# Combining of groups nine units apart instead of eleven, deeper rings for stored rows and weights, first units between the last products

## The chip, the cores and the metric

One Trainium2 chip, of which the kernel uses one core. The metric is the device time of one execution in microseconds (us), from the runtime's own count; a profiled execution also has a span, from its first to its last instruction. The engines of the core are named as the profile names them: PE (TensorE), DVE (VectorE), ACT (ScalarE), POOL (GpSimd) and SP (SyncE, which here only issues transfers).

## The reference

Inputs are x (8192 x 128) and adj (8192 x 8192), all float32. A layer norm of x goes through a graph layer whose weights are a function of adj, and the result through a mixture of 16 experts of which each row takes two.

```python
def _L0_gnn_ref(z, dist_matrix, W, B):
    msg = z @ W + B
    sens = sensitivity(dist_matrix, MU, SIGMA)      # exp(-(1/r - 1/mu)**2 / (2 sigma**2))
    weights = jnp.where(dist_matrix < CUTOFF, sens, 0.0)
    return weights @ msg

def _L0_ffn_ref(x, gate_w, gate_b, w1, b1, w2, b2, gamma, beta):   # E=16, K=2, H=128, F=256
    gate_logits = x @ gate_w + gate_b
    topk_vals, topk_idx = jax.lax.top_k(gate_logits, K)
    topk_w = jax.nn.softmax(topk_vals, axis=-1)
    h = jax.nn.relu(jnp.einsum('bsh,ehf->bsef', x, w1) + b1)
    expert_out = jnp.einsum('bsef,efh->bseh', h, w2) + b2
    sel = jnp.take_along_axis(expert_out, topk_idx[:, :, :, None], axis=2)
    y = x + jnp.sum(topk_w[..., None] * sel, axis=2)
    return layernorm(y) * gamma + beta

x = x + _L0_gnn_ref(_layernorm(x), adj, L0_gnn_W, L0_gnn_B)
x = x + _L0_ffn_ref(_layernorm(x)[None], ...)[0]
```

## The kernel before

The 8192 rows are 16 groups of 512. **The graph stage** takes group after group: 16 chunks of adj (512 rows x 512 columns, 1 MB) go through a ring of 8 buffers; DVE masks and squares (L614, L620), ACT takes a logarithm and an exponential (L488, L493), PE turns the chunk (L1078), ACT writes the weights (L499), and `products` on PE (L1059) adds weights times messages into one PSUM bank, two steps (`BEHIND`) after the turn. Two steps make a chunk, 32 a group. While a group runs, the gate of the group before is computed in slots between the steps (`gate_slot`): a second layer norm, the gate's logits, the two best experts, the row that each pair (row, expert) gets in a table sorted by expert, and eight indirect DMAs on POOL (L454) that scatter the normalised rows to `rows_in`.

**The expert stage** follows for all groups. The sorted rows are cut into 188 units of 128 rows, each of one expert, in four batches (63, 55, 39 and 31 units, of 6, 5, 3 and 2 groups). Unit `u` goes through these steps, each an in-order queue of its engine:

- SP `load_rows` (L352) reads its 64 KB from `rows_in`, 14 units ahead (`RIN`).
- DVE `fetch` (L923) copies the expert's first weights out of the resident table into one of `SLOTS` buffers, `AHEAD` units ahead; every 16 units it first reads the experts' numbers into registers (a TENSOR_LOAD, L917).
- PE `turn_tile` (L1097), four units ahead; ACT `copy_rows` (L552); PE `hidden` (L1108), two ahead; ACT `relu_hidden` (L561); PE `output` (L1136); DVE `add_bias` (L932), which writes the result into one of `RO` buffers, each for a pair of units; SP `store_rows` (L365) stores a pair (128 KB) to `rows_out`. `add_bias` of a pair waits until the store that last used its buffer has landed.

**Combining** brings the results back, a group at a time. POOL gathers the group's rows with eight indirect DMAs (L472) into one of 4 buffers; it begins a batch's first group when all stores of that batch have landed. SP reads the kept rows of the group (L376). `combine_slot(g, m)` then does ten steps m = 0 to 9 on DVE and ACT, one per unit, behind the unit's own instructions in the same queues: two weighted additions on DVE (L947, four instructions each), statistics (L626, L633), a reciprocal root (ACT L505, L507, and DVE L641 to L645), a shift (L961), the scaling on ACT (L573, four instructions), gamma (L966) and the last addition (L971). SP stores the group (L380).

**What sets the order.** Every engine runs one loop over `i`; unit `i`'s instructions come first and then those of `combine_slot(g, i - starts[g])`. `starts` is a list computed once: a group starts no earlier than `COMBINE_WAIT` = 14 units after its batch, and no earlier than `COMBINE_PACE` units after the group before. With 11 that gives 77, 88, 99, 110, 121, 132, 143, 154, 165, 176, 187, 198, 209, 220, 231, 242. Iterations from 188 on have no units in them, only combining.

```python
starts.append(max(at, starts[-1] + COMBINE_PACE) if starts else at)   # at = UNIT0[b + 1] + COMBINE_WAIT
```

The last products of the graph stage (steps 30 and 31 of group 15) stand on PE ahead of the first turns and hidden layers of the units. DVE's first fetches stand ahead of `gate_sum` (L706), which copies the last sum out of PSUM.

## Time and profile before

| | us |
|---|---|
| median of three runs | 1753.15 (1749.15 to 1754.33) |
| the profiled execution, its own time | 1751.72 |
| its span | 1750.0 |
| last turn of the graph stage on PE begins | 1466.33 |
| first unit's output on PE begins | 1475.57 |
| first combining begins | 1559.71 |
| last unit's bias begins | 1697.90 |
| last combining begins | 1738.76 |

Busy shares over the whole span are PE 92%, DVE 87%, ACT 91% and POOL 29%; they are averages over a graph stage of some 1470 us, which the change leaves alone up to its last two steps, and an expert stage of some 280 us. Times in the trace count from the span's start. A row of the timeline has its start, its length, the engine, the line, the operation with what it writes and reads, the number of merged instructions, and in brackets how long its engine was idle before it and what ended that. Names such as `chunk` and `msg` stand for the memory in which the expert stage's buffers are carved (`ro`, `slots`, `rin`, `back`, `zs`, `fin` in chunk; `rT`, `hT` in msg).

### The profile page before, as it was taken

How to read it: one execution, taken by the hardware profiler on the slowest of the kernel's cores; microseconds unless marked ns; L12 is line 12 of the kernel's file. 1: busy time of each engine (PE TensorE's matmuls, PEld its weight loads, DVE VectorE, ACT ScalarE, POOL GpSimd, SP SyncE). 2: the span in 40 equal slices, each digit the busy share in tenths (PEclk: the TensorE clock that was granted, in tenths of full speed). 3: DMA queues.
4: the chain of work that ended last, by engine and by line, in shares of the span. 5: the costliest groups of instructions: out<-in, count | busy, mean ns of one | idle time of the engine just before them, and what ended most of it. 6: DMA issues, size and time to landing. Idle time of an engine off the chain costs nothing.

```text
span 1750.0 us, 25339 instructions
## 1 busy us (share of the span) xinstructions
PE 1615.9 (92%) x8350; PEld 1074.9 (61%) x8350; DVE 1524.9 (87%) x2435; ACT 1598.6 (91%) x1749; POOL 514.8 (29%) x344
## 2 busy tenths in 40 slices
PE   4889999999999998999999999999999989998970
PEld 3556666666656565666665656556666656997860
DVE  7999989899999999989899999998989894576876
ACT  5889999999999999899999999989999986786862
POOL 1001040404041415050505050505050512156773
PEclk9999999999999999999999999999999999999995
DMA  9447876766666667576666676756676742466762
GB/s 320 146 139 251 247 212 197 218 197 209 200 203 200 203 201 217 172 216 198 205 198 211 196 214 192 225 171 209 198 216 197 225 118 61 134 171 192 203 169 83
DMA packets 228927, 338.30 MB, mean 193 GB/s; under 512 B 19200, under 2 KB 86272, under 8 KB 228672
## 3 DMA queue, kind: packets, MB, share of 16 engines
q1 hardware_dynamic: 220480, 319.63, 61.8%
q0 software_dynamic: 8320, 17.06, 3.3%
q8 instruction: 70, 1.15, 0.3%
q14 instruction: 57, 0.47, 0.1%
HBM read 303.07 MB, written 33.55 MB: 192 GB/s over the span
## 4 chain that ended last, share of the span: by engine, by line
PE 50%; ACT 21%; DVE 18%; issue 7%; POOL 2%; DMA 1%; DVEq 0%; SPq 0%; ACTq 0%; POOLq 0%
PE acc L1059 26%; PE tp L1078 13%; ACT chunk L488 8%; ACT chunk L493 6%; DVE chunk L614 6%; DVE chunk L620 5%; ACT wT L499 5%; PE tp L1108 4%; PE tp L1136 2%; PE acc L1136 2%; POOL spread L442 2%; DVE stats L626 2%; PE tp L1097 1%; DVE chunk L947 1%; PE misc L1011 1%
## 5 line engine op out<-in xcount | busy, mean ns | idle before, releaser
L1059 PE MATMUL acc<-wT,msg 128*128 128x512 f32 x2048 | 972.2, 597 | 0.0
L499 ACT ACTIVATE wT<-tp 128x1024 f32<-128x1024 f32 x512 | 751.8, 1468 | 30.3 <-PE tp L1078 30.2
L620 DVE SCALAR_TENSOR_TENSOR chunk<-chunk 128x2048 f32<-128x2048 f32 x256 | 584.8, 2284 | 65.6 <-ACT chunk L493 65.2
L1078 PEld LDWEIGHTS tp<-ident,chunk 128*128 128x128 f32 x4096 | 481.4, 142 | 224.7 <-issue 214.2
L488 ACT ACTIVATE chunk<-chunk 128x2048 f32<-128x2048 f32 x256 | 604.1, 2360 | 11.9 <-DVE chunk L614 11.9
L493 ACT ACTIVATE chunk<-chunk 128x2048 f32<-128x2048 f32 x256 | 605.8, 2367 | 0.0
L614 DVE SCALAR_TENSOR_TENSOR chunk<-chunk 128x2048 f32<-128x2048 f32 x256 | 583.8, 2281 | 2.3 <-DMA chunk<-in_adj_dram 2.3
L1078 PE MATMUL tp<-ident,chunk 128*128 128x128 f32 x4096 | 535.7, 274 | 0.0
L1059 PEld LDWEIGHTS acc<-wT,msg 128*128 128x128 f32 x2048 | 351.1, 191 | 252.8 <-issue 249.7
L454 POOL DMA_INDIRECT rows_in<-y,row_now x128 | 281.8, 2202 | 44.6 <-issue 44.6
L435 POOL TENSOR_TENSOR pool_carrier<-pool_carrier 1x1 f32<-1x1 f32 x32 | 10.3, 323 | 730.1 <-DVE row_now L791 707.8
L442 POOL TENSOR_SCALAR spread<-mv_now 128x4 f32<-128x4 f32 x16 | 53.4, 3339 | 394.8 <-DVE mv_now L633 394.8
L561 ACT ACTIVATE msg<-tp,chunk 128x128 f32<-128x128 f32 x376 | 117.8, 367 | 26.5 <-PE tp L1108 25.6
L472 POOL DMA_INDIRECT chunk<-rows_out,row_back x128 | 125.2, 978 | 39.1 <-issue 36.6
L1108 PE MATMUL tp<-msg,chunk 128*128 128x128 f32 x752 | 115.9, 277 | 0.0
L1108 PEld LDWEIGHTS tp<-msg,chunk 128*128 128x128 f32 x752 | 99.8, 193 | 0.0
L552 ACT ACTIVATE msg<-tp 128x128 f32<-128x128 f32 x188 | 51.9, 277 | 25.7 <-PE tp L1097 25.1
L923 DVE COPY chunk<-blobs 128x258 f32 x188 | 56.7, 304 | 17.7 <-ACT msg L561 14.8
L1136 PE MATMUL acc<-blobs,msg 128*128 x376 | 60.3, 283 | 9.6 <-DVE chunk L932 7.0
L1136 PE MATMUL tp<-blobs,msg 128*128 x376 | 60.6, 284 | 8.8 <-ACT msg L561 4.6
L1136 PEld LDWEIGHTS acc<-blobs,msg 128*128 128x128 f32 x376 | 49.8, 193 | 13.4 <-issue 12.6
L1136 PEld LDWEIGHTS tp<-blobs,msg 128*128 128x128 f32 x376 | 50.2, 194 | 12.6 <-issue 12.1
(112 smaller groups left out, 740.5 us busy)
## 6 DMA issues: line engine op xcount, KB each, us to landing
chunk<-in_adj_dram SPq DMA_DIRECT2D x256, 1024.0 KB, 5.4
chunk<-rows_in SPq DMA_DIRECT2D x188, 64.0 KB
rows_out<-chunk SPq DMA_DIRECT2D x92, 128.0 KB
y_kept<-y SPq DMA_DIRECT2D x16, 256.0 KB, 6.1
rows_in<-zeros SPq DMA_DIRECT2D x64, 64.0 KB
chunk<-y_kept SPq DMA_DIRECT2D x16, 256.0 KB
out_dram<-chunk SPq DMA_DIRECT2D x16, 256.0 KB, 2.7
blobs<-in_L_ffn_w_dram SPq DMA_DIRECT2D x1, 2048.0 KB, 11.7
```

The lines of the kernel that those rows point to most:

```text
L454: pool.indirect_dma_start(rows_in, bass.IndirectOffsetOnAxis(row_now[:, k, b:b + 1].bitcast(U32), 0), y[:, b, :], None).then_inc(scattered ...
L472: pool.indirect_dma_start(back[g % BACK][:, kb, :], None, rows_out[b], bass.IndirectOffsetOnAxis(row_back[:, g, kb:kb + 1].bitcast(U32), 0 ...
L488: act.activation(slot(c), slot(c), ACT.Ln, bias=TINY).then_inc(logged, 1)
L493: act.activation(slot(c), slot(c), ACT.Exp, scale=-1.0).then_inc(inverted, 1)
L499: act.activation(wT[:, (g * PPG + m) % WSLOTS, :], tp[(g * PPG + m) % TSLOTS][:, :], ACT.Exp, scale=-2.0).then_inc(weighted, 1)
L561: ins = act.activation(hT[u % HT][:, t * n:(t + 1) * n], h_bank[u % H_BANKS][:, t * n:(t + 1) * n], ACT.Relu, bias=slots[u % SLOTS][:, B1 ...
L614: dve.scalar_tensor_tensor(out=slot(c), in0=slot(c), scalar=1.0, in1=slot(c), op0=ALU.is_lt, op1=ALU.mult).then_inc(masked, 1)
L620: dve.scalar_tensor_tensor(out=slot(c), in0=slot(c), scalar=2.0, in1=slot(c), op0=ALU.subtract, op1=ALU.mult).then_inc(squared, 1)
L1059: ins = pe.matmul(acc[:, :], msg[:, n, :], wT[:, (g * PPG + m) % WSLOTS, k * ROWS:(k + 1) * ROWS], start=(n == 0), stop=(n == 2 * PPG - 1))
L1078: ins = pe.transpose(tp[s % TSLOTS][:, t * ROWS + b * P:t * ROWS + (b + 1) * P], chunk[:, c % RING, b, j:j + P], ident[:, :])
L1108: ins = pe.matmul(h_bank[u % H_BANKS][:, t * n:(t + 1) * n], slots[u % SLOTS][:, W1 + t * P:W1 + (t + 1) * P], rT[u % RT][:, 0:n], start=T ...
L1136: ins = pe.matmul(o_bank[u % O_BANKS][:, r:r + D], hT[u % HT][:, t * n + r:t * n + r + P], blobs[:, bass.ds(second_layers[u], 1), W2 + t * ...
```

## The change

Four constants and the place of two pieces of work:

- `COMBINE_PACE` goes from 11 to 9. `starts` becomes 77, 86, 95, 104, 113, 122, 132, 141, 150, 159, 168, 177, 186, 195, 204, 213. SP's loads of the kept rows (at `starts[g] - COMBINE_PACE`) come nine units ahead instead of eleven.
- `RO` goes from 4 to 8 pairs of stored rows, `SLOTS` from 9 to 12 and `AHEAD` from 7 to 8.
- On PE, the products of the last two steps stand between the turns of units 0 to 3 and the hidden layers of units 0 and 1.

```diff
-        SLOTS, RIN, RT, HT, RO, BACK, ZS, FIN = 9, 14, 4, 4, 4, 4, 3, 2
+        SLOTS, RIN, RT, HT, RO, BACK, ZS, FIN = 12, 14, 4, 4, 8, 4, 3, 2
...
-        AT_ONCE, AHEAD = 16, 7
+        AT_ONCE, AHEAD = 16, 8
...
-        COMBINE_WAIT, COMBINE_PACE, COMBINE_LONG = 14, 11, 10
+        COMBINE_WAIT, COMBINE_PACE, COMBINE_LONG = 14, 9, 10
...
-            for m in range(PPG - BEHIND, PPG):
-                products(GROUPS - 1, m)
-
...
-            for u in range(TURN_LEAD):
-                turn_tile(u)
-            for u in range(HIDDEN_LEAD):
-                hidden(u)
+            turn_tile(0)
+            turn_tile(1)
+            products(GROUPS - 1, PPG - 2)
+            turn_tile(2)
+            turn_tile(3)
+            hidden(0)
+            products(GROUPS - 1, PPG - 1)
+            hidden(1)
```

PE at the seam of the two stages, before: after the last turn (L1078) all six remaining products (L1059), then four turns of units (L1097), the hidden layers of two (L1108, two instructions each), unit 4's turn and unit 2's hidden layer.

```order
1129 L1078 MATMUL tp<-ident,chunk 128x128 x8
1130 L1059 MATMUL acc<-wT,msg 128x512 x6
1131 L1097 MATMUL tp<-ident,chunk 128x128 x4
1132 L1108 MATMUL tp<-msg,chunk 128x128 x4
1133 L1097 MATMUL tp<-ident,chunk 128x128
1134 L1108 MATMUL tp<-msg,chunk 128x128 x2
```

PE at the same place in the changed kernel, where L1097 has become L1094 and L1108 L1105:

```order
1129 L1078 MATMUL tp<-ident,chunk 128x128 x8
1130 L1059 MATMUL acc<-wT,msg 128x512 x2
1131 L1094 MATMUL tp<-ident,chunk 128x128 x2
1132 L1059 MATMUL acc<-wT,msg 128x512 x2
1133 L1094 MATMUL tp<-ident,chunk 128x128 x2
1134 L1105 MATMUL tp<-msg,chunk 128x128 x2
1135 L1059 MATMUL acc<-wT,msg 128x512 x2
1136 L1105 MATMUL tp<-msg,chunk 128x128 x2
```

The four turns and the first hidden layer moved ahead of the last products; the second hidden layer stands behind them as before.

DVE between two groups' combining late in the stage (groups 8 and 9), before: the last step of one group (L971), two more units' bias (L932) and fetch (L923), then the first step of the next group (L947).

```order
2020 L971 TENSOR_TENSOR chunk<-chunk,xs 128x512
2021 L932 ISA
2022 L932 TENSOR_TENSOR chunk<-tp,blobs 128x128
2023 L923 ISA
2024 L923 COPY chunk<-blobs 128x258
2025 L932 ISA
2026 L932 TENSOR_TENSOR chunk<-acc,blobs 128x128
2027 L923 ISA
2028 L923 COPY chunk<-blobs 128x258
2029 L947 SCALAR_TENSOR_TENSOR chunk<-chunk,share 128x128 x4
```

DVE in the changed kernel, between groups 9 and 10:

```order
2003 L966 TENSOR_TENSOR chunk<-chunk,gamma_bc 128x512
2004 L932 ISA
2005 L932 TENSOR_TENSOR chunk<-acc,blobs 128x128
2006 L917 TENSOR_LOAD e_tab
2007 L923 ISA
2008 L923 COPY chunk<-blobs 128x258
2009 L971 TENSOR_TENSOR chunk<-chunk,xs 128x512
2010 L947 SCALAR_TENSOR_TENSOR chunk<-chunk,share 128x128 x4
```

The last step of a group and the first of the next now stand in the same unit's place, with no unit between them that carries no combining. At the end of the loop, three whole groups (13, 14 and 15) stand behind the last unit instead of five.

## Rows read from the trace of the kernel before

**Rows 1.** Busy time by stage: start:end, us, then each engine's busy us
```profile
1475.50:1560.00 84.50, 82.55 (x723) 81.21 (x724) 50.75 (x227) 65.85 (x235) 19.01 (x23) 1.00 0.48 136
1560.00:1697.00 137.00, 120.85 (x974) 114.06 (x973) 100.89 (x444) 105.71 (x381) 99.63 (x112) 0.98 0.71 193
```
**Rows 2.** Timeline of DVE: the first step of groups 0 to 4, 10 and 15
```profile
1559.71 1.14 DVE L947 SCALAR_TENSOR_TENSOR chunk<-chunk,share 128x128 f32<-128x128 f32 x4 [0.50 <-DMA chunk<-rows_out,row_back]
...
1572.44 1.12 DVE L947 SCALAR_TENSOR_TENSOR chunk<-chunk,share 128x128 f32<-128x128 f32 x4
...
1590.99 1.13 DVE L947 SCALAR_TENSOR_TENSOR chunk<-chunk,share 128x128 f32<-128x128 f32 x4
...
1603.19 1.13 DVE L947 SCALAR_TENSOR_TENSOR chunk<-chunk,share 128x128 f32<-128x128 f32 x4
...
1621.38 1.12 DVE L947 SCALAR_TENSOR_TENSOR chunk<-chunk,share 128x128 f32<-128x128 f32 x4
...
1696.86 1.13 DVE L947 SCALAR_TENSOR_TENSOR chunk<-chunk,share 128x128 f32<-128x128 f32 x4
...
1738.76 2.31 DVE L947 SCALAR_TENSOR_TENSOR chunk<-chunk,share 128x128 f32<-128x128 f32 x8
```
**Rows 3.** Timeline at the end: last unit's bias and store, last step of group 15
```profile
1697.90 0.28 DVE L932 TENSOR_TENSOR chunk<-acc,blobs 128x128 f32<-128x128 f32 x1
...
1698.49 0.47 SPq L365 DMA_DIRECT2D rows_out<-chunk  x1
...
1746.49 0.69 DVE L971 TENSOR_TENSOR chunk<-chunk,xs 128x512 f32<-128x512 f32 x1
```
**Rows 4.** Timeline of POOL: last gather of group 0, batches two and four
```profile
1556.94 0.94 POOL L472 DMA_INDIRECT chunk<-rows_out,row_back  x1 [0.30 <-issue]
...
1618.47 0.18 POOL L435 TENSOR_TENSOR pool_carrier<-pool_carrier 1x1 f32<-1x1 f32 x1 [8.54 <-DMA rows_out<-chunk]
...
1700.43 0.94 POOL L472 DMA_INDIRECT chunk<-rows_out,row_back  x1 [0.30 <-issue]
1702.78 0.18 POOL L435 TENSOR_TENSOR pool_carrier<-pool_carrier 1x1 f32<-1x1 f32 x1 [1.41 <-DMA rows_out<-chunk]
...
1724.51 0.94 POOL L472 DMA_INDIRECT chunk<-rows_out,row_back  x1 [0.30 <-issue]
```
**Rows 5.** Timeline of all engines at the seam, and two units behind it
```profile
1467.21 5.32 PE L1059 MATMUL acc<-wT,msg 128*128 128x512 f32 x12
...
1472.56 0.69 DVE L706 COPY yT<-acc 128x512 f32<-128x512 f32 x1 [10.90 <-PE acc L1059]
...
1475.57 0.71 PE L1136 MATMUL tp<-blobs,msg 128*128 x4 [0.50 <-ACT msg L561]
...
1483.12 0.61 PE L1136 MATMUL acc<-blobs,msg 128*128 x4
...
1484.12 0.61 PE L1136 MATMUL tp<-blobs,msg 128*128 x4
```
**Rows 6.** Who waited for whom, 1560 to 1697: us, times, longest
```profile
DVE chunk L966 <- ACT chunk L573: 8.4, 9, 1.3
DVE chunk L923 <- ACT msg L561: 8.2, 7, 3.1
DVE chunk L932 <- PE tp L1136: 6.9, 14, 1.3
...
DVE chunk L932 <- DMA rows_out<-chunk: 6.0, 2, 4.0
DVE chunk L932 <- PE acc L1136: 3.7, 9, 0.7
```
**Rows 7.** Timeline of DVE: a unit's bias that waited for a store
```profile
1586.74 0.29 DVE L932 TENSOR_TENSOR chunk<-acc,blobs 128x128 f32<-128x128 f32 x1 [4.01 <-DMA rows_out<-chunk]
...
1587.15 0.68 DVE L966 TENSOR_TENSOR chunk<-chunk,gamma_bc 128x512 f32<-128x512 f32 x1
```
**Rows 8.** DVE's register loads: duration in ns, minimum, median and longest
```profile
L917 DVEq TENSOR_LOAD <-e_tab x15: 310/1312/3654, 1458.3 to 1676.3; - x15
```

More of the change, by code:

```diff
@@ L1139, in output @@
                 ins.then_inc(o_full, 1)
-            for u in range(TURN_LEAD):
-                turn_tile(u)
-            for u in range(HIDDEN_LEAD):
-                hidden(u)
+            assert BEHIND == 2 and T_BANKS == 2 and TURN_LEAD == 4 and HIDDEN_LEAD == 2
+            turn_tile(0)
[6 more added lines that the diff above has]
+            hidden(1)
             for i in range(NU):
```

## The prediction, made before the changed kernel ran

> **What bounds the kernel now.** The change begins at the seam of the two stages, so I read the trace from there. First the busy time by stage [rows 1]. From the first unit to the first combining (77 units, 84.5 us) PE is busy 82.55 us: PE bounds, and an undisturbed unit takes 1.00 us, as two successive outputs show (1483.12, 1484.12) [rows 5]. From 1560 to 1697 the other 111 units share their queues with combining. There PE is busy 120.9 of 137 us, ACT 105.7, DVE 100.9 and POOL 99.6. No engine is full.
>
> Next the starts of groups [rows 2], which show the real pace. Eleven units take 12.73 us from group 0 to 1, 12.20 from 2 to 3, and on average (1696.86 - 1621.38) / 6 = 12.58 from 4 to 10: 12.58 / 11 = 1.144 us a unit. Two intervals stand out: 18.55 us from group 1 to 2 and 18.19 from 3 to 4. Then the table of waits for this stage [rows 6], which says what DVE, on which all combining hangs, waits for: ACT's scaling (8.4 us), something before a fetch (8.2), PE's outputs (6.9 + 3.7), and stores of rows (6.0 in two waits).
>
> Behind the last unit's bias (1697.90) come 52.1 us without PE [rows 3]. From group 10's start to group 15's are (1738.76 - 1696.86) / 5 = 8.38 us a group [rows 2]: one group's chain over DVE and ACT with nothing beside it. POOL finishes gathering group 15 at 1724.51 + 0.94 = 1725.45 [rows 4], but DVE takes it up at 1738.76. So the end is set by the chain of groups that are left over, not by gathers.
>
> **1. The seam.** Before, PE runs six product instructions in a row to 1467.21 + 5.32 = 1472.53, while ACT and DVE have nothing to do (DVE was idle for 10.90 us), and the first output starts at 1475.57 [rows 5], 3.04 us later. Now four turns and one hidden layer are inside the products. What PE must do behind the last product is hidden layer 1, turn 4, hidden layer 2. A unit is one turn and two pairs of matmuls in 1.00 us, so a turn is about 0.1 us and a pair about 0.45: 0.45 + 0.1 + 0.45 = 1.0 us. What moved ahead costs PE 4 x 0.1 + 0.45 = 0.85 us, by which the last product ends later. 3.04 - 0.85 - 1.0 = 1.2 us are saved at most, and nothing if a copy on ACT is late. The copies are 0.3 us pieces that have a product's 1.8 us to run in, so I take 1.1. The sum leaves PSUM 0.85 us later (L706), but the second output, which waits for it, comes after that anyway.
>
> **2. Deeper rings.** A bias waited 4.01 us for a store at 1586.74 [rows 7], and all such waits are 6.0 us [rows 6]. With four pairs a store has eight units to land; with eight it has sixteen. 6.0 us go. The check from elsewhere: the interval around them was 18.55 - 12.58 = 6.0 us too long. If the waits only move, it is 0. SLOTS and AHEAD I cost at nothing: the 8.2 us before fetches, for which the table names ACT, are the size of DVE's register loads, which last 1.31 us each and 3.65 at most [rows 8] and stay, in the same number. The eighth fetch (0.3 us) is covered by DVE's idle 10.90 us.
>
> **3. The pace inside the units.** 111 units held 10.1 groups at eleven apart and hold 12.3 at nine. What does a period of nine units cost? DVE: 100.9 / 10.1 = 10.0 us busy a period. Two units less take away 2 x 0.41 (1586.74 to 1587.15 is one bias and one fetch [rows 7]), which leaves 9.2. ACT's scaling keeps it waiting 8.4 / 10.1 = 0.8 us, register loads 8.2 / 10.1 x 9 / 11 = 0.7. Together 10.7 us. Its waits for PE (10.6 / 10.1 = 1.0 us) come on top or vanish, since DVE now runs with less slack. POOL: the eight groups 6 to 13 were gathered from 1618.47 to 1701.37, 10.36 us a group [rows 4], just under 10.7. PE needs 9.0, ACT less than DVE. So the bounds are 10.4 and 11.7, and I take 10.7 because DVE is nearest to full: 10.7 / 9 = 1.189 us a unit, 0.045 more than now, over 111 units **5.0 us lost** (2 to 17 between the bounds).
>
> The last bias starts at 1697.9 - 1.1 - 6.0 + 5.0 = 1695.8.
>
> **4. Behind the last unit.** Three whole groups are left, not five. DVE's chain alone would reach group 15 some 3 x 8.4 = 25 us after the last bias. But group 14 can't be gathered before the last stores land. POOL starts them at 1702.78, 4.9 us after the last bias, and is done at 1725.45, 22.7 us later [rows 4]. A gather lands some 1.8 us after its issue: group 0's last one ended its issue at 1557.88, and DVE, which waited for it, began at 1559.71 [rows 2, 4]. 4.9 + 22.7 + 1.8 = 29.4 us: what is late next is POOL, by 4 us over DVE's chain. From group 15's start to the end of the span are 1750.0 - 1738.76 = 11.2 us, as before. 29.4 + 11.2 = 40.6 instead of 52.1: **11.5 us saved**. Is POOL free by then? Group 13's gather ended 82.9 us after batch two's began; that beginning moves with the units to about 1612, so to 1695, before 1695.8 + 4.9.
>
> **The sum.** 1695.8 + 40.6 = 1736.4, that is 13.6 us less than 1750.0. Against the profiled execution's own time that is 1751.72 - 13.6 = 1738.1 us. Its time is 1.4 us below the median of the runs, so for the median 1739.5.
>
> **A rule of the Trainium skill that speaks against it.** The 128 gathers take POOL 0.94 us with 0.30 between them, the same beside units (1556.94) as in the tail, where no fetches run (1724.51) [rows 4]. The Trainium skill, "SBUF — State Buffer", section "SBUF: two separate sides", says of DMAs issued from GpSimd that a fp32 SBUF-to-SBUF copy on VectorE locks it out of the port they share, and puts such a DMA at about 3.1 us instead of 0.62. By it a denser DVE would stretch the gathers. The trace doesn't agree here, so the sum goes by the row.
>
> **The rivals.** *Combining doesn't overlap with units.* If DVE can do nothing useful in a group's chain, nine units cost 9 x 0.41 + 8.38 = 12.1 us, 1.341 a unit: 21.9 us lost in place of 5.0. The last bias comes at 1712.7, the span is 1753.3, and the median about 1756, slower than before. It decides from 11.8 us a period on, where the loss (18.6) eats all savings. Against it: by the same rule eleven units would cost 4.5 + 8.4 = 12.9, and three views of them gave 12.2 to 12.7. That is not far.
>
> *Gathers are held up by a busier DVE.* Let each wait for one DVE instruction of 0.28 us: 8 x 0.28 more is 12.6 us a group, and nine units can't go faster: 1.40 us a unit, 28 us lost instead of 5, and 2 x 2.2 more in the tail. The median would be about 1767. Against it stands the even 0.94.
>
> *The waits for stores stay.* Gathers, kept rows and results of a group are as many bytes in nine units as in eleven, so transfers are denser. If stores take that much longer, 6.0 us aren't saved: 1745.5.
>
> *The pace is nominal.* DVE keeps all its waits for PE, a period costs 11.1 to 11.7: 1744 to 1752.
>
> *More is gained.* The interval from group 3 to 4 was 5.6 us too long [rows 2], with the one register load of 3.65 us in it [rows 8]. If such a pause doesn't come again, or DVE and POOL run at 10.4 a period: 1731 to 1735.
>
> **How the numbers follow.** The forecast (1735 to 1744) gets 0.50, the nominal pace 0.17, the stores 0.10, more gained 0.15, no overlap 0.05, held-up gathers 0.03. The likeliest gives 1739.5. The range takes in the bounds of the pace, the stores and the gained pause: 1730 to 1749, which leaves out about 0.15. A measurement of this kernel can tell some 0.3% (5.3 us) from no change. Faster by more than that, below 1747.9: 0.91. Within it: 0.05. Slower: 0.04.
>
> **What would show it.** The first output starts 1.1 us earlier, with ACT's copies between products. No wait of a bias for a store is left. Groups start 10.4 to 11 us apart where they were 12.6. Behind the last bias DVE does two and a half groups and then waits some 4 us for the last gathers, which it never did; about 41 us lie between that bias and the end. I am wrong if periods are near 12, if the table of waits has DVE wait for gathers in the middle of batches, or if the clock that PE is granted falls in the unit stage for longer than before, which no term here has in it.

## The result, and the profile after

| | before | changed | ratio with its 95% interval |
|---|---|---|---|
| median of the runs, first comparison | 1751.68 us (6 runs) | 1745.18 us (6 runs) | 0.9961 [0.9947, 0.9974] |
| second comparison, another chip | 1750.90 us (11 runs) | 1745.43 us (6 runs) | 0.9966 [0.9954, 0.9978] |
| profiled execution: its own time | 1751.72 us | 1745.93 us | |
| its span | 1750.0 us | 1744.2 us | |

The changed kernel is faster by 6.5 us in the first comparison and by 5.5 us in the second: just more than the 0.3% that can be told from no change, and less than half of the 13.6 us that were forecast. The median lies inside the predicted range, 5.7 us above the forecast of 1739.5 and above the band of 1735 to 1744 that had most of the chance. The trace of the changed kernel tells which term took the rest, in the order of the prediction.

**The seam.** The timeline of all engines there (start, length, engine, line):

```profile
1465.05 1.04 PE L1078 MATMUL tp<-ident,chunk 128*128 128x128 f32 x8
...
1467.95 0.45 ACT L552 ACTIVATE msg<-tp 128x128 f32<-128x128 f32 x2 [0.81 <-PE tp L1094]
...
1470.24 1.88 PE L1059 MATMUL acc<-wT,msg 128*128 128x512 f32 x4
...
1472.96 0.61 PE L1133 MATMUL tp<-blobs,msg 128*128 x4
```

The second row is one of ACT's copies, now between products, the third is the last products, and the first output (fourth row) starts 7.91 us after the last turn of the stage before it; before it was 9.24 us. That is 1.3 us saved, where 1.1 was expected. The first bias comes 2.7 us earlier in all (1473.72 instead of 1476.42); the other 1.3 to 1.4 us were already there before the seam, in a part that the change doesn't touch, and are a difference between two executions.

**The unit stage.** The first steps of groups 0, 3, 4, 5, 6 and 12 on DVE, and the last bias:

```profile
1557.15 1.14 DVE L947 SCALAR_TENSOR_TENSOR chunk<-chunk,share 128x128 f32<-128x128 f32 x4
...
1592.93 1.12 DVE L947 SCALAR_TENSOR_TENSOR chunk<-chunk,share 128x128 f32<-128x128 f32 x4
...
1606.73 1.13 DVE L947 SCALAR_TENSOR_TENSOR chunk<-chunk,share 128x128 f32<-128x128 f32 x4
...
1622.27 1.14 DVE L947 SCALAR_TENSOR_TENSOR chunk<-chunk,share 128x128 f32<-128x128 f32 x4
...
1635.16 1.13 DVE L947 SCALAR_TENSOR_TENSOR chunk<-chunk,share 128x128 f32<-128x128 f32 x4
...
1704.06 1.14 DVE L947 SCALAR_TENSOR_TENSOR chunk<-chunk,share 128x128 f32<-128x128 f32 x4
...
1706.36 0.28 DVE L932 TENSOR_TENSOR chunk<-acc,blobs 128x128 f32<-128x128 f32 x1
```

Compare [rows 2]. From group 0 to 3 a period of nine units takes (1592.93 - 1557.15) / 3 = 11.9 us, from group 6 to 12 (1704.06 - 1635.16) / 6 = 11.5 us. The forecast had 10.7. (From group 5 to 6 are ten units, since group 6 begins the second batch; they take 12.9 us.) The pause around groups 3 to 5 has come again: its two periods, 13.8 and 15.5 us, are together some 5.8 us above two ordinary ones, as before (5.6). From the first bias to the last the stage takes 232.6 us where it took 221.5: 11.1 us more. No wait for a store is left in it. If the 6.0 us of these waits were given back in full, the pace took 17.1 us, not 5.0. The periods alone say nearly the same: (11.48 / 9 - 12.58 / 11) x 111 = 14.6 us, and 1.3 us for the three longer periods at the start.

The windows view (start:end, length, busy us of PE, PE's weight loads, DVE, ACT and POOL, granted clock, DMA share, GB/s) for the whole of the combining and for its even part, groups 6 to 12, answers to [rows 1]:

```profile
1557.00:1705.00 148.00, 125.39 (x983) 115.67 (x982) 111.31 (x492) 109.62 (x396) 105.23 (x115) 0.99 0.71 191
1635.00:1704.00 69.00, 60.36 (x480) 55.61 (x479) 53.99 (x240) 53.61 (x194) 50.85 (x56) 1.00 0.71 193
```

And the table of DVE's waits in that even part (us in all, times, longest), against [rows 6]:

```profile
DVE chunk L966 <- ACT chunk L573: 5.7, 6, 1.3
DVE chunk L932 <- PE acc L1133: 4.0, 9, 0.7
DVE chunk L932 <- PE tp L1133: 2.4, 7, 0.6
DVE chunk L923 <- issue: 1.0, 2, 0.7
DVE chunk L923 <- ACT msg L561: 0.9, 1, 0.9
```

By six groups: DVE is busy 9.0 us a period (forecast 9.2), waits 0.95 us for the scaling (0.8), 0.3 us for register loads (0.7; the table names them "issue" and ACT's msg), and **(4.0 + 2.4) / 6 = 1.07 us for PE's outputs**, as much as before (1.0) with two units fewer in the period. This is what the forecast let vanish. PE is busy 60.36 / 6 = 10.1 us a period, more than DVE; the forecast had put it at 9.0.

**Behind the last unit.** POOL's and SP's timelines at the end of the units, and the first steps of groups 13 to 15 with group 15's last:

```profile
1705.42 1.58 SPq L365 DMA_DIRECT2D rows_out<-chunk  x2
1707.05 0.43 SPq L380 DMA_DIRECT2D out_dram<-chunk  x1
...
1708.54 0.18 POOL L435 TENSOR_TENSOR pool_carrier<-pool_carrier 1x1 f32<-1x1 f32 x1 [7.81 <-DMA rows_out<-chunk]
...
1730.16 1.11 POOL L472 DMA_INDIRECT chunk<-rows_out,row_back  x1 [0.30 <-issue]
```

```profile
1712.48 2.31 DVE L947 SCALAR_TENSOR_TENSOR chunk<-chunk,share 128x128 f32<-128x128 f32 x8
...
1722.70 2.33 DVE L947 SCALAR_TENSOR_TENSOR chunk<-chunk,share 128x128 f32<-128x128 f32 x8 [1.75 <-DMA chunk<-rows_out,row_back]
...
1732.97 2.31 DVE L947 SCALAR_TENSOR_TENSOR chunk<-chunk,share 128x128 f32<-128x128 f32 x8 [1.78 <-DMA chunk<-rows_out,row_back]
...
1740.71 0.69 DVE L971 TENSOR_TENSOR chunk<-chunk,xs 128x512 f32<-128x512 f32 x1
```

POOL waited 7.81 us for the last stores (before 1.41 [rows 4]), gathered for 22.7 us, and DVE, which never waited for gathers behind the last unit before, waits for them now, 1.75 and 1.78 us. Groups 14 and 15 come 10.2 and 10.3 us after the one ahead: POOL's rate of 10.36 us, not DVE's chain of 8.4. From the last bias to the end are 37.8 us, where it was 52.1: 14.3 us saved (forecast 11.5).

The sum: 2.7 (of which the seam 1.3) - 11.1 + 14.3 = 5.9 us earlier, which is the spans' 5.8 us but for rounding.

### The profile page after: what moved, and what is told of

Same layout as the page of the kernel before. It is cut to its first block, busy times and chain, and to the rows that moved or that the text cites. A ratio compares the mean times of both kernels' runs of the same rounds, so it can differ in the third digit from the quotient of the medians.

```text
span 1744.2 us, 25343 instructions
## 1 busy us (share of the span) xinstructions
PE 1617.0 (93%) x8350; PEld 1075.8 (62%) x8350; DVE 1522.5 (87%) x2435; ACT 1597.1 (92%) x1749; POOL 515.0 (30%) x344
## 4 chain that ended last, share of the span: by engine, by line
PE 63%; DVE 22%; ACT 7%; issue 4%; POOL 2%; DMA 1%; DVEq 0%; SPq 0%; POOLq 0%; ACTq 0%
PE acc L1059 33%; PE tp L1078 17%; DVE chunk L614 8%; DVE chunk L620 7%; PE tp L1105 4%; PE tp L1133 3%; PE acc L1133 2%; ACT chunk L488 2%; ACT wT L499 2%; ACT chunk L493 2%; POOL spread L442 2%; DVE stats L626 1%; PE tp L1094 1%; PE misc L1011 1%; DVE y L727 1%
## 5 line engine op out<-in xcount | busy, mean ns | idle before, releaser
L1059 PE MATMUL acc<-wT,msg 128*128 128x512 f32 x2048 | 969.5, 596 | 0.0
L499 ACT ACTIVATE wT<-tp 128x1024 f32<-128x1024 f32 x512 | 737.5, 1440 | 29.3 <-PE tp L1078 29.0
L1078 PEld LDWEIGHTS tp<-ident,chunk 128*128 128x128 f32 x4096 | 482.0, 142 | 222.9 <-issue 212.0
L488 ACT ACTIVATE chunk<-chunk 128x2048 f32<-128x2048 f32 x256 | 597.2, 2333 | 12.0 <-DVE chunk L614 12.0
L493 ACT ACTIVATE chunk<-chunk 128x2048 f32<-128x2048 f32 x256 | 598.9, 2339 | 0.0
L1078 PE MATMUL tp<-ident,chunk 128*128 128x128 f32 x4096 | 536.7, 275 | 0.0
L1059 PEld LDWEIGHTS acc<-wT,msg 128*128 128x128 f32 x2048 | 350.9, 192 | 250.5 <-issue 248.0
L435 POOL TENSOR_TENSOR pool_carrier<-pool_carrier 1x1 f32<-1x1 f32 x32 | 10.9, 342 | 734.2 <-DVE row_now L791 705.5
L1105 PE MATMUL tp<-msg,chunk 128*128 128x128 f32 x752 | 116.0, 277 | 0.0
L1105 PEld LDWEIGHTS tp<-msg,chunk 128*128 128x128 f32 x752 | 99.6, 193 | 0.5 <-issue 0.5
L1133 PE MATMUL tp<-blobs,msg 128*128 x376 | 61.8, 287 | 18.6 <-DVE chunk L932 7.9
L923 DVE COPY chunk<-blobs 128x258 f32 x188 | 55.9, 300 | 15.9 <-issue 8.0
L1133 PE MATMUL acc<-blobs,msg 128*128 x376 | 60.0, 283 | 5.7 <-ACT msg L561 2.4
L1133 PEld LDWEIGHTS tp<-blobs,msg 128*128 128x128 f32 x376 | 49.9, 193 | 24.8 <-issue 24.0
L1133 PEld LDWEIGHTS acc<-blobs,msg 128*128 128x128 f32 x376 | 49.9, 193 | 9.4 <-issue 8.9
## 6 DMA issues: line engine op xcount, KB each, us to landing
blobs<-in_L_ffn_w_dram SPq DMA_DIRECT2D x1, 2048.0 KB, 11.7
```

What stands on the lines that cost most here:

```text
L488: act.activation(slot(c), slot(c), ACT.Ln, bias=TINY).then_inc(logged, 1)
L493: act.activation(slot(c), slot(c), ACT.Exp, scale=-1.0).then_inc(inverted, 1)
L499: act.activation(wT[:, (g * PPG + m) % WSLOTS, :], tp[(g * PPG + m) % TSLOTS][:, :], ACT.Exp, scale=-2.0).then_inc(weighted, 1)
L1059: ins = pe.matmul(acc[:, :], msg[:, n, :], wT[:, (g * PPG + m) % WSLOTS, k * ROWS:(k + 1) * ROWS], start=(n == 0), stop=(n == 2 * PPG - 1))
L1078: ins = pe.transpose(tp[s % TSLOTS][:, t * ROWS + b * P:t * ROWS + (b + 1) * P], chunk[:, c % RING, b, j:j + P], ident[:, :])
L1105: ins = pe.matmul(h_bank[u % H_BANKS][:, t * n:(t + 1) * n], slots[u % SLOTS][:, W1 + t * P:W1 + (t + 1) * P], rT[u % RT][:, 0:n], start=T ...
```

## Why DVE still waits for PE

In the even part DVE is busy 78% of the time and PE 87%, and yet both wait. The reason stands in the outputs of one period, group 8's. First PE's timeline, outputs alone (L1133), then what DVE does at the same time:

```profile
1658.20 0.71 PE L1133 MATMUL acc<-blobs,msg 128*128 x4
...
1660.25 0.71 PE L1133 MATMUL tp<-blobs,msg 128*128 x4 [0.79 <-ACT msg L561]
...
1661.70 0.71 PE L1133 MATMUL acc<-blobs,msg 128*128 x4 [0.19 <-DVE chunk L932]
...
1668.31 0.61 PE L1133 MATMUL acc<-blobs,msg 128*128 x4
1670.16 0.71 PE L1133 MATMUL tp<-blobs,msg 128*128 x4 [0.68 <-ACT msg L561]
```

```profile
1657.66 0.28 DVE L932 TENSOR_TENSOR chunk<-acc,blobs 128x128 f32<-128x128 f32 x1
...
1658.06 0.69 DVE L971 TENSOR_TENSOR chunk<-chunk,xs 128x512 f32<-128x512 f32 x1
1658.66 1.14 DVE L947 SCALAR_TENSOR_TENSOR chunk<-chunk,share 128x128 f32<-128x128 f32 x4
1659.71 0.28 DVE L932 TENSOR_TENSOR chunk<-tp,blobs 128x128 f32<-128x128 f32 x1
...
1661.16 0.28 DVE L932 TENSOR_TENSOR chunk<-acc,blobs 128x128 f32<-128x128 f32 x1
```

There are two output banks, and a bank is free again when DVE has added its bias. At 1658.06 DVE begins the last step of one group and goes straight on to the first of the next, 1.65 us, which the order of instructions ahead of the prediction already showed side by side. Only then comes the bias that frees the bank tp (1659.71 to 1659.99), and 0.26 us later the output that needs this bank (1660.25), 2.05 us after the one at 1658.20. The row names ACT, but the relu that this output needs, by the order two iterations back, was long done; the next output follows its bank's bias by the same 0.26 us (1661.16 + 0.28, then 1661.70), and there the row names DVE. The next takes 1.45 us (DVE's second addition), then come units of 1.0 to 1.2 us, and at the end one of 1.85 us beside ACT's scaling, where the row names ACT and nothing here proves more. The nine distances from 1658.20 to 1670.16 are 11.96 us: nine units at 1.00 us, 2.35 us more in the three long places (1.05, 0.45 and 0.85) and 0.6 us spread over the other six. In the short units PE is the slower one and DVE waits for it. Time lost in a long place isn't made up in a short one, since PE can run only two outputs ahead. So, by this reading, **a period is the sum, over its units, of the slowest engine's share in each**, not the largest of the engines' sums over the period. Eleven units had two short places more; taking them away and putting two steps into one place saved 12.58 - 11.48 = 1.1 us a period, not the 1.9 us of the forecast.

That is a reading. It says that a third output bank would let short units make up for long ones, and the experiments put that to the test.

## The experiments

The first eight runs were on two chips on which every kernel took some 130 us longer, the one before too (1884.11 and 1878.83 us). The traces of the variants show the excess in the unit stage (351 to 365 us long), in pauses while POOL issues indirect DMAs; the kernel before has no trace there, and the changed kernel itself didn't run there. Each is therefore compared with the kernel before on its own chip, and periods are read between the pauses, where POOL issues next to nothing; these are periods *without* gathers beside them. The last four experiments were again on a chip like the first comparison's.

### Eleven apart with all else changed

```diff
-        COMBINE_WAIT, COMBINE_PACE, COMBINE_LONG = 14, 9, 10
+        COMBINE_WAIT, COMBINE_PACE, COMBINE_LONG = 14, 11, 10
```

> The changed kernel with groups eleven units apart again; rings and seam stay changed. Theory 1 (the closer pace gave back in the units what it saved behind them): rings and seam alone give what the whole change gave, some 1.3 + 6 us, so 1744 to 1745, with periods of about 12.6 us a group, no wait for stores, and 52 us behind the last bias. Theory 2 (the pace did save, and the rings did not): 1750 to 1751.

Measured: 1880.43 us against 1884.11 for the kernel before, ratio 0.9980 [0.9971, 0.9989]. Behind the last bias are 52.0 us, as before the change: the 14.3 us at the end belong to the pace alone. No bias is shown waiting for a store. The time, 3.7 us below before, is that of neither theory; the rest of the question was lost in this chip's pauses, so the kernel was run once more on another:

> The changed kernel with groups eleven units apart again, a second time, because in the first the expert stage of every kernel, the one before too, was 130 us longer than in the runs that the prediction is about. Theory 1 (the closer pace gave back in the units what it saved behind them): 6 to 7 us faster than before, as the whole change. Theory 2 (the pace saved, the rings did not): 1 to 2 us faster than before.

1878.57 us against 1878.83, ratio 0.9996 [0.9987, 1.0005]: 0.3 us below before, nearer to theory 2, but the same pauses were there and it decides nothing. What they look like, in one window of the first of the two and in DVE's and PE's timelines:

```profile
1553.00:1594.00 41.00, 12.25 (x72) 10.74 (x70) 4.34 (x19) 4.65 (x16) 30.75 (x36) 0.59 0.31 78
```

```profile
1587.82 0.29 DVE L932 TENSOR_TENSOR chunk<-acc,blobs 128x128 f32<-128x128 f32 x1 [18.84 <-remote]
...
1588.36 1.22 PE L1133 MATMUL acc<-blobs,msg 128*128 x4 [17.17 <-DVE chunk L932]
```

While POOL is busy 31 of 41 us, DVE is busy 4 and PE 12, and one bias starts 18.84 us late, released by something that the trace doesn't name ("remote"). It isn't DVE alone: a copy on ACT starts 13.37 us late there (1591.21). POOL's gathers have a median of 0.947 us, as in the first comparison (0.945 before). What makes these pauses is open, and no reading here rests on them.

### Ten apart

```diff
-        COMBINE_WAIT, COMBINE_PACE, COMBINE_LONG = 14, 9, 10
+        COMBINE_WAIT, COMBINE_PACE, COMBINE_LONG = 14, 10, 10
```

> The changed kernel with ten units between groups: the last step of a group and the first of the next are no longer in one unit's place. Theory 1 (what hurts is the place that holds both, and the lack of a unit without combining in which the engines catch up): a period of about 11.5 us for ten units, so 1.15 a unit where nine gave 1.30; the last bias near 1695, four and a bit groups of 8.4 us and 11.2 us behind it, 1740 to 1742. Rival (DVE has a fixed sum of work and waits for a period, whatever stands where): ten units take 11.7 + 0.4 = 12.1 us, the last bias comes at 1700 and the time is 1745 to 1747.

1880.72 us against 1884.11, ratio 0.9985 [0.9976, 0.9994], with 43.7 us behind the last bias. Its periods of ten units without gathers are 11.7, 13.8, 12.7 and 11.2 us, the 13.8 with the pause that is told of at the end. The interval overlaps those of nine and eleven apart: on that chip the pace makes no difference that can be measured. Inconclusive as to which is best.

### The rings as they were

```diff
-        SLOTS, RIN, RT, HT, RO, BACK, ZS, FIN = 12, 14, 4, 4, 8, 4, 3, 2
+        SLOTS, RIN, RT, HT, RO, BACK, ZS, FIN = 9, 14, 4, 4, 4, 4, 3, 2
...
-        AT_ONCE, AHEAD = 16, 8
+        AT_ONCE, AHEAD = 16, 7
```

> The changed kernel with RO 4, SLOTS 9 and AHEAD 7 as before; pace nine and the new seam stay. If the stores' waits were a cost of their own (6.0 us before), they come back, longer at the denser pace: 1751 or more, and the table of waits shows DVE L932 waiting for stores for 5 us or more. If they only took the place of other waits: 1745 to 1746.

1881.15 us against 1884.11, ratio 0.9984 [0.9975, 0.9993].

> The changed kernel with RO 4, SLOTS 9 and AHEAD 7 as before, a second time for the same reason. If waits for stores are a cost of their own, they come back at 5 us or more and the time is within 2 us of before; if they only take the place of other waits, 6 to 7 us faster than before.

1878.15 us against 1878.83, ratio 0.9997 [0.9988, 1.0006]. The times are 3.0 and 0.7 us below before, the second as expected if waits for stores come back. But in neither trace is such a wait named, though RO is 4 again; and a store that was late would not be seen among the pauses, where the releaser has no name. Whether the rings save 6.0 us by themselves **stays open**. What is known is that the waits of [rows 7] are in the trace of before and in neither trace of the changed kernel.

### A third output bank

```diff
-        o_bank = [third[:, ROWS:ROWS + UW], acc[:, 0:UW]]
+        o_bank = [third[:, ROWS:ROWS + UW], acc[:, 0:UW], misc[:, 0:UW]]
+        def out_bank(u):
+            return o_bank[u % O_BANKS if u < UNITS[0] else u % 3]
...
-                if u >= O_BANKS:
+                if u >= UNITS[0] + 3:
+                    pe.wait_ge(ro_ready, u - 2)
+                elif u >= UNITS[0]:
+                    pe.wait_ge(ro_ready, u)
+                elif u >= O_BANKS:
                     pe.wait_ge(ro_ready, u - O_BANKS + 1)
```

The output's matmul and the bias use out_bank(u). The misc bank is free from the second batch on, which begins with unit 63, ahead of the first combining. The pace is nine.

> The changed kernel, but from the second batch on the outputs of the units go round three PSUM banks (misc is the third, free by then) where there were two, so PE may be three outputs ahead of the bias on DVE. Theory 1a (PE is tied to single long places of DVE by the two banks): the period of nine units in batches two to four falls from 11.7 towards 10.7 us, 5 to 8 us in all, and the time is near 1739. Rival 1b (DVE and ACT are full over the whole period, or PE is held up by ACT): no change, 1745, periods of 11.5 to 11.8.

1875.25 us against 1884.11, ratio 0.9956 [0.9944, 0.9968].

> The changed kernel with the outputs of units in three PSUM banks from the second batch on, a second time for the same reason. Theory 1a (PE is tied to single long places of DVE by the two banks): the period of nine units falls from 11.7 towards 10.7 us in batches two to four, and the time is 12 to 14 us below before. Rival 1b (DVE or ACT is full over the period): 6 to 7 us below before, periods of 11.3 to 11.8.

1873.49 us against 1878.83, ratio 0.9975 [0.9962, 0.9989]. It is 8.9 and 5.3 us below before, less than the 12 to 14 that were expected; but on both chips it was faster than the same pace with two banks and the old rings, by 5.9 and 4.7 us. The periods show where. Here are two periods of nine units, from one group's first step to that of the second group behind it (1753.13 to 1773.88 us), as a window with its busy times and as DVE's waits in it. The added lines have shifted the bias to L935, the first step to L950 and the output to L1140:

```profile
1753.10:1773.90 20.80, 19.83 (x163) 18.64 (x161) 17.91 (x84) 17.68 (x67) 0.29 (x2) 0.99 0.56 157
```

```profile
DVE chunk L935 <- PE acc L1140: 1.0, 2, 0.8
DVE chunk L969 <- ACT chunk L576: 1.0, 2, 0.6
DVE chunk L926 <- issue: 0.7, 1, 0.7
```

The same two views with two banks and nine units (the old rings' first run, same chip), between the first steps at 1750.43 and 1774.46 us:

```profile
1750.40:1774.50 24.10, 20.50 (x164) 18.81 (x162) 18.41 (x84) 18.43 (x69) 1.25 (x2) 1.00 0.46 128
```

```profile
DVE chunk L966 <- ACT chunk L573: 2.2, 2, 1.1
DVE chunk L932 <- PE acc L1133: 1.1, 2, 0.6
DVE chunk L923 <- issue: 1.1, 2, 1.0
DVE chunk L932 <- PE tp L1133: 0.8, 2, 0.5
```

10.4 us a period against 12.0, with the same work on DVE (8.96 and 9.2 us busy), granted clocks of 0.99 and 1.00, and POOL all but idle in both. The waits for PE are 0.5 us a period instead of 0.95, those for the scaling 0.5 instead of 1.1. PE is busy 95% of the time with three banks and 85% with two. From group 7 on, the periods without gathers are, with three banks, seven from 10.0 to 10.4 us and one of 11.0 (both runs), with two banks 12.0, 12.0, 11.3, 11.1 and 12.2, 12.0, 11.8, 11.0 (the old rings' two runs). So there the two-deep coupling holds PE and DVE back by 1 us or more in nine units. These four periods, 5.4 and 5.2 us shorter in sum, are about the whole gain: in the two periods from group 2 to 4, also without gathers, three banks take 24.1 and 23.7 us together and two banks 23.6 and 23.4. DVE's waits for PE are shorter there too (0.7 and 0.3 us against 2.1 and 2.0), but those ahead of a fetch and for the scaling are longer by as much (5.0 and 5.4 against 3.2 and 3.3). Why isn't shown.

Where it gains, this speaks for the reading by places: nothing was taken away from any engine, only the distance by which one may run ahead of the other. The rings differ between the two runs as well. Against them as the cause stands that neither window has a wait for a store, and that the changed kernel, with the new rings and two banks, has periods of 11 to 12 us; but a pair that differs in the bank alone is missing.

### A quarter of the scaling

```diff
-                    for b in range(TB):
+                    for b in range(1):
                         ins = act.activation(zs[g % ZS][:, b, :], zs[g % ZS][:, b, :], ACT.Identity,
```

> The changed kernel with three of the four scaling instructions of each group left out (ACT L573 scales only 128 of 512 rows, so the output is wrong in the others): ACT's work in that unit's place falls by 3 x 0.42 = 1.25 us. If ACT is what a period waits for (rival 1b, ACT's side), periods fall by 1.2 us or more, from 11.7 to 10.5. If DVE's two long places at a group's start set it (theory 1a), they fall by 0.5 us or less, since DVE's wait for the scaling (0.9 us a group) goes but PE has no more to do in it.

1870.13 us (4 runs) against 1878.83, ratio 0.9951 [0.9934, 0.9967]. From group 7 on, the periods without gathers are 11.6, 10.2, 10.2 and 9.9 us, on average 1.25 us shorter than with all of the scaling and the old rings on the same chip. That is as much as the rival had expected, and more than the 0.5 us that theory 1a allowed: DVE's places alone don't set the period. ACT isn't full (7.1 to 9.1 us busy in these periods), yet three instructions less in one place of a period shorten it: a long place on ACT holds the others up as well.

### The changed kernel again, on the last chip

> The changed kernel itself beside the kernel before, under the conditions of the experiments, in which the expert stage is some 130 us longer. Theory 1 (pace gives in the tail and takes in the units): undisturbed periods of nine units are 11 to 12 us, as in the first trace, 38 us lie behind the last bias, and the time is that of old_rings within 2 us, 0 to 4 us below before. Rival: the ratio of the first comparison (6.5 us) holds here too.

1745.43 us against 1750.90, ratio 0.9966 [0.9954, 0.9978]. The long pauses weren't there, so the rival came true, and with it the periods and the end that theory 1 named. Periods of 11.1 to 12.5 us but for three around the pause (13.5, 14.1, 15.7), 37.8 us behind the last bias, no wait for a store. The profile of the changed kernel repeats itself, and the pause with it: a register load takes 3.91 us at 1599.6 us, 3.66 in the first trace.

### Half of the gathers

```diff
-                    for kb in range(KB):
+                    for kb in range(TB):
                         pool.indirect_dma_start(
...
-                    dve.wait_ge(back_in[g % BACK], (g // BACK + 1) * KB * 16)
-                if m in (0, 1):
+                    dve.wait_ge(back_in[g % BACK], (g // BACK + 1) * TB * 16)
+                if m == 0:
```

> The changed kernel with the second expert's rows left out of combining: four gathers a group instead of eight, and one weighted addition (L947) instead of two, so the output lacks the second expert. In the traces of the experiments a unit takes 3.6 to 4.9 us while POOL issues gathers and 1.4 otherwise, where the first traces had 1.2 to 1.3 in both. If the gathers' issue is what holds the units up, half of them take half of the 130 us away: 60 to 70 us less than the changed kernel. If something else in the stage does (code, the stores, the clock), it is 10 to 20 us less, by the 1.05 us of DVE for each group and the shorter gathers behind the last unit.

1728.10 us (4 runs), ratio to the kernel before 0.9870 [0.9855, 0.9884], 17.3 us less than the changed kernel on this chip. The unit stage takes 222.7 us instead of 233.7 and the tail 30.5 instead of 37.8. The pauses of the other chips, which it was to explain, weren't there, so that question stays open. Its first periods are 11.6, 10.7 and 12.4 us: with half of POOL's gathers gone, and one of DVE's two additions with them, nine units take 10.4 us or more throughout. POOL's rate doesn't bound the units; it does bound the tail. In the even part, groups 6 to 12, the periods are on average 0.5 us shorter than the changed kernel's on this chip, though 1.1 us of DVE's work is gone.

### A quarter of the additions

```diff
-                    for b in range(TB):
+                    for b in range(1):
                         ins = dve.scalar_tensor_tensor(out=z[:, b, :], in0=back[g % BACK][:, m * TB + b, :],
```

> The changed kernel with three of the four instructions left out of each weighted addition (L947 works on 128 of 512 rows; the others keep y alone, so the output is wrong there): DVE's long places at a group's start fall from 1.45 to 0.65 us, its work by 6 x 0.26 = 1.6 us a group. Theory 1a (these places hold PE up through the two banks): undisturbed periods fall from 11.7 to 10.5 or less. Rival 1c (ACT's scaling place alone holds PE up): they stay above 11.

1731.49 us (4 runs), ratio 0.9898 [0.9883, 0.9913], 13.9 us less than the changed kernel. DVE's six missing instructions are some 0.28 us each, 1.7 us a period, and the six even periods go from 11.1 to 11.8 us on the same chip to between 9.6 and 10.9: 0.8 to 1.5 us each, 1.05 on average. Two of the six are below the 10.5 us of theory 1a and none is above the 11 of rival 1c. The sizes of this run and the last fit the reading by places. By it, leaving out the second addition can give back only the 0.45 us that its place took over a plain unit, and half of the gathers gave 0.5 us. For this run the estimate is 0.45 us, and 3 x 0.28 = 0.84 us in the place of two steps, 1.3 us together, and 1.05 were measured. A full DVE would have given back its whole work, 1.1 and 1.7 us. (The other run also left out gathers, so it isn't a pure test.) The tail stays at 37.9 us, though DVE has less to do in it: the tail is POOL's, as the waits for gathers said.

### A third bank and ten apart

The edits of the third bank and of ten apart together.

> Third bank for outputs and ten units between groups. With PE freed from DVE's long places, a period is DVE's own sum: 10.3 us for nine units and 10.3 to 10.8 for ten. If so ten apart has undisturbed periods of 10.8 us or less, more units a us than nine, and the time lies 0 to 4 us above or below third_bank (four groups of 8.4 us behind the last bias against three). If DVE's sum doesn't hold, periods are 11.5 or more.

**1734.94 us (5 runs, 1734.0 to 1737.07), ratio to the kernel before 0.9914 [0.9901, 0.9927]: faster than both kernels, by 16.0 and 10.5 us.** The first steps of its last two groups within the units and of group 15, a window over its units and combining, and DVE's waits for PE there:

```profile
1676.84 1.13 DVE L950 SCALAR_TENSOR_TENSOR chunk<-chunk,share 128x128 f32<-128x128 f32 x4
...
1687.21 1.13 DVE L950 SCALAR_TENSOR_TENSOR chunk<-chunk,share 128x128 f32<-128x128 f32 x4
...
1721.72 2.31 DVE L950 SCALAR_TENSOR_TENSOR chunk<-chunk,share 128x128 f32<-128x128 f32 x8 [0.81 <-DMA chunk<-rows_out,row_back]
```

```profile
1557.00:1687.00 130.00, 117.98 (x991) 112.52 (x990) 103.35 (x467) 106.31 (x393) 94.09 (x105) 1.00 0.75 206
```

```profile
DVE chunk L935 <- PE tp L1140: 2.4, 4, 1.2
DVE chunk L935 <- PE acc L1140: 2.4, 6, 0.6
DVE chunk L935 <- PE misc L1140: 1.7, 4, 0.5
```

The last two groups within the units start 10.4 us apart, the four periods ahead of that are 10.8 to 11.4 us, each with ten units and with gathers beside them: less than the changed kernel's 11.5 for nine, though only the last two are within the 10.8 us that were expected. Only in the first half are they longer, 11.3 to 12.9. DVE's waits for PE are 6.5 us in all, where the changed kernel on the same chip has 14.2 (8.1 + 6.1). The unit stage takes 214.3 us instead of 233.7. The tail is 44.7 us instead of 37.8, as one more group is left over, and it is nearly even between DVE's chain and POOL: three distances of 8.4 us, and then one of 9.3 with a wait of 0.81 us for gathers. One more thing is in its gain: between groups 1 and 6 it has periods of 12.3 to 12.9 us but none like the changed kernel's 13.5 to 15.7. At unit 118, where the pause sits, DVE waits 2.05 us ahead of the fetch and 0.40 for the output, where it was 3.81 and 3.35: up to 4.7 us of the 10.5 may be this. Whether it is the bank's doing, the pace's or neither's is open. How much of the 10.5 us is the bank's and how much the pace's isn't separated: on this chip neither ran alone. A fourth bank wasn't tried.

## Why the prediction was right and wrong

1. **The seam: right.** 1.1 us expected, 1.3 seen, by the mechanism told: copies between products, one turn and two hidden layers behind them.
2. **The rings: seen as predicted, not proven.** The 6.0 us of waits for stores are gone in both traces of the changed kernel. That the rings did it, and not the new spacing, the old rings' run was to show and couldn't; its traces name no wait for a store either.
3. **The pace: this step failed.** It lost 17.1 us, where 5.0 were forecast. The composition was nearly right: DVE's busy time (9.2 forecast, 9.0 seen) and its waits for the scaling and register loads (1.5 together, 1.3 seen) hold. Wrong was the choice that its 1.0 us of waits for PE "come on top or vanish, since DVE now runs with less slack". They stayed at 1.07 us. The reason given for the choice, "DVE is nearest to full", misread [rows 1]: PE is busy 120.9 us there and DVE 100.9. And "PE needs 9.0" took the time of an undisturbed unit; by the same rows PE is busy 120.9 / 111 x 9 = 9.8 us in nine units, and 10.1 were seen. DVE isn't the full engine of a period that could be filled up to its brim; between two engines that are two outputs apart, each waits for the other within one period, by turns. The rival *the pace is nominal* named just this, with 11.1 to 11.7 us a period and 1744 to 1752 us: it is what happened (11.5 us, 1745.2), with a chance of 0.17 where the choice of 10.7 had most of 0.50. The evidence was there: [rows 6] had DVE waiting for PE with neither full (74% and 88% busy). The order of instructions ahead of the prediction also showed the last step of one group and the first of the next in one unit's place, and the prediction gives this no price; it is 1.65 us in the trace. The size follows: (11.5 - 10.7) x 111 / 9 = 9.9 us on top of the 5.0, and of the rest, some 2 us, 1.3 are in the first three periods, which are 11.9 us and not 11.5.
4. **Behind the last unit: mechanism right, size off by 2.8 us.** POOL's gathers are late next, 22.7 us, landing 1.7 us later, and 11.2 us behind them: each as forecast. Off was the time from the last bias to POOL's start, 2.2 us (1706.36 to 1708.54) instead of 4.9. Before, SP issued a result and kept rows right ahead of the last store [rows 3 shows the store alone, at 1698.49]; now the last two stores go first and the result's issue comes behind them (1705.42, 1707.05). That fits a store that isn't queued behind larger transfers. But POOL's gathers of group 13 also ran beside that store before [rows 4, 1700.43], and now their last ended at 1700.73, ahead of it; no experiment took the two apart. The wait of DVE for gathers, forecast as one of some 4 us, is 1.75 + 1.78 = 3.5 us in two pieces.
5. **The pause from group 3 to 5: stayed,** as the sum assumed (5.6 before, 5.8 after). It sits at unit 118, the first of the third batch, on DVE and on PE (last section). The rival *more is gained* had it go.
6. **The other rivals.** *No overlap* (12.1 us a period) fell by 0.6 us in the even part only: the 11.5 measured lie nearer to it than to the 10.7 of the forecast, more than its chance of 0.05 said. *Held-up gathers*: not seen. The prediction's "even 0.94" is the usual length and not that of all: single gathers take up to 1.45 us beside units and 1.40 in the tail. But in the changed kernel the 112 beside units have a mean of 0.99 us and the 16 in the tail 1.00 (before: 0.98 and 0.98), so the trace doesn't agree with the Trainium skill, "SBUF — State Buffer", section "SBUF: two separate sides", in the changed kernel either. *Stores' waits stay*: no.
7. **The sum.** Forecast 1.1 + 6.0 - 5.0 + 11.5 = 13.6 us. Seen 1.3 + 6.0 - 17.1 + 14.3 = 4.5, and 1.3 to 1.4 us from the stage before, which isn't the change's. That the time still fell into the range is in part luck: the pace cost 12.1 us more than forecast, and the end, for a reason that isn't known, gave 2.8 us more. That the clock would be no matter was right: 0.99 over the combining, 0.98 before [rows 1].

## What to carry to other kernels

When several engines take turns over small buffers, work out a period unit by unit, taking in each unit's place the slowest engine, and let a wait vanish only if the buffer between the two engines is deep enough to carry the short places over the long one. An engine's sum over the period is a lower bound, and here DVE's, 9.0 us busy, was 2.5 us below the 11.5 measured, and PE's, 10.1, was 1.4 below. Before one packs work closer in time, ask how deep the coupling is: here one more output bank with ten units between groups gave 16.0 us over the old kernel, where nine units with two banks gave 5.5.

## What the hardware showed beside that

- In every trace of this case the longest wait of DVE ahead of a fetch is that of unit 118, the first of the third batch, where DVE loads the experts' numbers into registers (2.0 to 3.8 us). The load took 3.66 and 3.91 us in two traces of the changed kernel (at 1599 to 1600 us), and 3.65 in that of before, where the median is about 1.3 [rows 8]. PE, which loads the same numbers, then stands still ahead of the output of unit 118. These two places make the two long periods from group 3 to 5; before, both lay in the interval from group 3 to 4. In the changed kernel, DVE's fetch, PE's output, and the piece of the chain that ended last:

```profile
1603.04 0.30 DVE L923 COPY chunk<-blobs 128x258 f32 x1 [3.56 <-issue]
...
1614.94 0.71 PE L1133 MATMUL tp<-blobs,msg 128*128 x4 [2.73 <-issue]
```

```profile
1599.47 3.41 DVEq L917
```

Why the load is longer there isn't known.

- On two of the chips, all kernels took some 130 us longer; the traces show it in the unit stage, with DVE released up to 20.3 us late while POOL issued indirect DMAs, whose own median length (0.95 us) was the same. The cause isn't known.
